# Attention unit in groups of three score steps and two split steps, and a second SBUF region moved to the first one's remainder by 512 bytes

## The chip, the cores and the metric

The kernel runs on one core of one Trainium2 chip. TensorE (PE in the profile) multiplies matrices, ScalarE (ACT) evaluates functions such as exp, VectorE (DVE) works elementwise, GpSimd (POOL) helps out, SyncE (SP) issues DMAs. The metric is the device time of one execution in microseconds. A kernel and its change are compared by the median of several executions.

## What is computed

One transformer block on `x` of 2 x 2048 tokens with 576 channels, conditioned by a vector per batch item. Cut to what matters here:

```python
h = modulate(rmsnorm(x, g1, D), scale_msa, shift_msa)
qkv = (h @ qkv_w.T + qkv_b).reshape(B, N, 3, 16, 36).transpose(2, 0, 3, 1, 4)
q, k, v = rmsnorm(qkv[0]) * 36 ** -0.5, rmsnorm(qkv[1]), qkv[2]
attn = softmax(einsum('bhqd,bhkd->bhqk', q, k))
o = einsum('bhqk,bhkd->bhqd', attn, v)
x = x + tanh(gate_msa) * (o @ proj_w.T + proj_b)
h2 = modulate(rmsnorm(x, g2, D), scale_mlp, shift_mlp)
x = x + tanh(gate_mlp) * (gelu(h2 @ fc1_w.T + fc1_b) @ fc2_w.T + fc2_b)
```

## The kernel before, in words

Everything is float32. A product that TensorE takes in its fast float32 form (fp32r) is made of two or three passes over a high and a low part of each operand, so most matmuls come as `hi` and `lo`.

There are three stages. The first makes q, k and v and stores them. The second, attention, ends at about 1882 us together with the first two output projections. The third, the feed-forward, runs over `NB` = 8 blocks of 512 tokens, and in each over 18 steps of a `fc1` and a `fc2`.

**A unit of attention** is one pair of heads against 512 queries; there are `NU` = 64, written out one after the other. It has 16 key steps `kt` of 128 keys.

- `score(u, kt)`, L1633: two matmuls (one for each head), weights from `kT`, moving operand `qT`, into one of `RING` = 3 slots of two PSUM banks. Before its first weight load it waits in `ring_free` until the exp of three entries earlier is done, since that exp reads the slot which the score overwrites.
- `exps(u, kt)`, L1248, on ScalarE, in the order of `kt`: one exp of 128 x 1024 out of the slot, into `p_r` for the eight split steps (`kt` 0 to 3 and 12 to 15) and into `prob` for the eight whole steps (4 to 11). Before the exp of step 6 ScalarE also copies out one half of the last unit's output (`take_ob`).
- `high_p`, `low_p`, L1446 and L1453, on VectorE: make `p_hi` and `p_lo` of a split step.
- `split_value(u, j)`, L1659: four matmuls of fp32r, weights `vx`, moving `p_hi` and `p_lo`; it waits for `low_p`, and the one with `j` = 0 also for the copies of the last unit's output (`take_oa`, `take_ob`), whose PSUM banks it restarts.
- `value(u, kt)`, L1649: two matmuls in full float32 for a whole step, all eight in a row at the unit's end.

The first four split steps of a unit (`j` 0 to 3) are multiplied in the unit itself, the last four in the next unit (`older(j)`). The order of all this on TensorE is the order of the calls in the loop `for u in range(NU)`; no scheduler moves anything. Semaphores alone tie the engines together. Around units 60 to 62 the projection of the first block (`proj(0, m)`) stands in between and takes a ring entry of its own.

**Memory.** `main_phase` lays its tensors in two regions of SBUF. The low one begins at `low_end` = 2816 bytes of each partition: `kT`, `vp`, `qT`, `prob`, and in the feed-forward `mh_hi`, `mh_lo`, `w1_hi`, `w1_lo`, `a_hi`, `a_lo`. The high one begins at `W2`, counted down from the top (`top` = 229312): the feed-forward weights `w2`, and in attention in the same place `p_hi`, `p_r`, `p_lo` and `vx`; below it, counted down from `W2`, the projection's weights `wp_hi`, `wp_lo` and inputs `o_hi`, `o_lo`. `low_end` leaves 256 when divided by 512, `W2` = 146368 leaves 448. The sizes of the tensors that the fp32r matmuls read, and the steps between their slices, are multiples of 512 bytes, so the whole high region reads at 448 and the low one at 256. In `fc2` (L1719) the weights lie in the high region and the moving operand in the low one.

Of the kernel before, what the change touches and what calls it, by code (L numbers as in the profile page):

```python
# [15 lines left out]
B, N, D = 2, 2048, 576  # L16
# [9 lines left out]
NT = N // P  # L26
FC = F // P
# [17 lines left out]
def wait(eng, sem, value):  # L45

    if isinstance(value, int) and value <= 0:
        return
    eng.wait_ge(sem, value)
# [33 lines left out]
def build(nc, xT, cT, ada, adan, adab, wqkv, qkvb, wp, pb, w1, f1b, w2, f2b, gains, outT):  # L83
# [7 lines left out]
    with ExitStack() as ctx:  # L91
        ps = ctx.enter_context(nc.psum_tensor("ps", [P, 8, 512], F32))

        def sb(stack, name, shape, dt=F32):
            return stack.enter_context(nc.sbuf_tensor(name, shape, dt, align_bytes=64 if np.prod(shape[1:]) >= P else 32))

        ident = sb(ctx, "ident", [P, P])
        ones = sb(ctx, "ones", [P, P], F32R)
        mod = sb(ctx, "mod", [P, 6, KC, B])
        gate_b = sb(ctx, "gate_b", [P, 2, KC, B])  # L100
        gain = sb(ctx, "gain", [P, 4])
        qscale = sb(ctx, "qscale", [P, 1])
        bound = sb(ctx, "bound", [P, 1])
        unbounded = sb(ctx, "unbounded", [P, 1], mybir.dt.int32)
        pb_t = sb(ctx, "pb_t", [P, KC])
        f2b_t = sb(ctx, "f2b_t", [P, KC])
        f1b_t = sb(ctx, "f1b_t", [P, FC])

        first = FirstUnit(nc, ctx, qk_hi, qk_lo, v_s, m_s)
        parts = qkv_phase(nc, ctx, sb, ps, first, xT, cT, ada, adan, adab, wqkv, qkvb, pb, f1b, f2b, gains, qk_hi, qk_lo, v_s, m_s,  # L110
                  ident, ones, mod, gate_b, gain, qscale, bound, unbounded, pb_t, f2b_t, f1b_t)
        main_phase(nc, ctx, ps, first, parts, qk_hi, qk_lo, v_s, m_s, l_s, oh_s, ol_s, xT, w2, wp, w1, outT, ident, ones, unbounded, bound, mod, gate_b,
                   gain, f1b_t)
# [720 lines left out]
def place(u):  # L834

    return u // C // B, u // C % B, u % C


def ring_of_step(n):

    return n + sum(n >= b for b in PROJ_BEFORE)
# [15 lines left out]
def main_phase(nc, ctx, ps, first_unit, parts, qk_hi, qk_lo, v_s, m_s, l_s, oh_s, ol_s, xT, w2, wp, w1, outT, ident, ones, unbounded, bound, mod, gate_b,  # L857
# [4 lines left out]

    top = nc.sbuf_top // 64 * 64
    low_end = first_unit.base
    W2 = top - 8 * FC * D
    WP = W2 - 4 * 2 * KC * DP
    OB = WP - 4 * (KC + KF) * BLK
    here = [low_end]

    def at(name, shape, dt, offset):  # L870
        return nc.alloc_sbuf_tensor_at(name, shape, dt, offset=offset)
# [5 lines left out]

    w2c = at("w2", [P, FC, 2 * D], F32R, W2)
    w2_raw = at("w2_raw", [P, FC, 2 * D], F32, W2)
    wp_hi = at("wp_hi", [P, KC, DP], F32R, WP)  # L880
# [4 lines left out]

    p_hi = at("p_hi", [P, HIGHS, 2 * BLK], F32R, W2)
    p_r = at("p_r", [P, NS, 2 * BLK], F32, W2 + 8 * HIGHS * BLK)
    p_lo = at("p_lo", [P, NS, 2 * BLK], F32R, W2 + 8 * HIGHS * BLK)
    VX = W2 + 8 * (HIGHS + NS) * BLK
# [170 lines left out]
    with nc.Block() as block:  # L1060
# [560 lines left out]
        def _(pe):  # L1621
            parts[4](pe)

            def ring_free(entry):

                before = entry - RING
                for m in range(KC):
                    if before == ring_of_proj(m):
                        pe.wait_ge(pgate_done, m + 1)
                        return  # L1630
                wait(pe, exp_done, before + 1 - sum(before > ring_of_proj(m) for m in range(KC)))

            def score(u, kt):  # L1633

                it, r, c = place(u)
                entry = ring_of_step(NT * u + kt)
                if kt == 0:
                    pe.wait_ge(q_ld[u % 2], QDMA * (u // 2 + 1))
                if u == 0 and kt == 2:
                    pe.wait_ge(first_unit.tqlo_done, B * NT)  # L1640
                if c == 0 and kt % TPB == 0:
                    pe.wait_ge(k_ld[r][kt // TPB], KDMA * (it + 1))
                ring_free(entry)
                for h in range(2):
                    mm = pe.matmul(ps[:, 2 * (entry % RING) + h, :], kT[r][:, h, kt * P:(kt + 1) * P], qT[:, u % 2, h],  # L1645
                                   start=True, stop=True)
                mm.then_inc(s_mm, 1)

            def value(u, kt):  # L1649

                it, r, c = place(u)
                j = kt - EARLY
                if c == 0 and j == 0:
                    pe.wait_ge(v_ld[r], 16 * (it + 1))
                pe.wait_ge(exp_done, NT * u + kt + 1)
                pe.matmul(OA[0:64], vp[r][:, kt, 0:64], prob[:, j, 0:BLK], start=False, stop=False)  # L1656
                pe.matmul(OBK[64:VW], vp[r][:, kt, 64:VW], prob[:, j, BLK:2 * BLK], start=False, stop=False).then_inc(fv_mm, 1)  # L1657

            def split_value(u, j):  # L1659

                r, q = u // C % B, NS * u + j
                if u % C == 0 and j == 0:
                    pe.wait_ge(v_split, 4 * (u // C + 1))
                if j == 0:
                    wait(pe, oa_evac, u)
                    wait(pe, ob_evac, u)
                pe.wait_ge(plo_done, q + 1)
                for h, out in enumerate((OA, OBK)):
                    for n, part in enumerate((p_hi[:, q % HIGHS], p_lo[:, j])):
                        mm = pe.matmul(out, vx[r][:, j, h], part[:, h * BLK:(h + 1) * BLK],  # L1670
                                       start=j == 0 and n == 0, stop=j == NS - 1 and n == 1)
                mm.then_inc(rv_mm, 1)

            def proj(i, m):

                if m == 0:
                    pe.wait_ge(o_ld, ODMA * (i + 1))
                if i == 0:
                    ring_free(ring_of_proj(m))
                elif i == 1 and m < 2:  # L1680
                    pe.wait_ge(exp_done, NT * NU)
                elif m == 0 and i > 1:
                    pe.wait_ge(nrm_done, i)
                elif m > 0:
                    pe.wait_ge(pgate_done, KC * i + m - (1 if i == 1 else 0))
                for k in range(KC):
                    parts = passes(k, wp_hi, wp_lo, o_hi, o_lo)
                    if m == KF:
                        parts = ((wp_hi, o_hi), (wp_hi, o_lo)) if k < KF else ((wp_hi, o_hi),)
                    for n, (w, a) in enumerate(parts):  # L1690
                        mm = pe.matmul(proj_bank(i, m), w[:, k, m * P:(m + 1) * P], a[:, k],  # L1691
                                       start=k == 0 and n == 0, stop=k == KF and n == len(parts) - 1)
                mm.then_inc(proj_mm, 1)
# [47 lines left out]
            for u in range(NU):  # L1741
                def older(j):

                    if u > 0:
                        split_value(u - 1, EARLY + j)

                score(u, 0)
                score(u, 1)
                older(0)
                score(u, 2)  # L1750
                older(1)
                score(u, 3)
                score(u, 4)
                older(2)
                score(u, 5)
                older(3)
                if u in (LAST + 1, LAST + 2):
                    proj(0, 2 * (u - LAST) - 1)
                for kt in range(6, 9):
                    score(u, kt)  # L1760
                split_value(u, 0)
                score(u, 9)
                split_value(u, 1)
                score(u, 10)
                score(u, 11)
                split_value(u, 2)
                if LAST <= u < LAST + 3:
                    if u == LAST:
                        pe.wait_ge(wplo_done, 2 * KC)
                    proj(0, 2 * (u - LAST))  # L1770
                score(u, 12)
                score(u, 13)
                split_value(u, 3)
                score(u, 14)
                score(u, 15)
                for kt in WHOLE:
                    value(u, kt)
            sum_rows(0)
# [76 lines left out]
```

## Time and profile before

| | |
|---|---|
| median of 3 executions | 2906.13 us (2906.03 to 2906.17) |
| the profiled execution | 2906.52 us |
| its span, first to last instruction | 2904.7 us |
| PE busy | 2880.2 us, 99% |
| DVE busy | 1968.6 us, 68% |
| ACT busy | 1578.1 us, 54% |
| granted TensorE clock, mean | 0.997 |

The profile's page has six parts: busy time of each engine, the span in 40 slices, DMA queues, the chain of work that ended last, the costliest groups of instructions, and DMA issues. The trace behind it answers in more detail; the view used most below is the timeline, where a row gives the start in us, the time from the first start to the last end, the engine, the line, the operation, the operands and how many instructions were merged. Matmuls overlap in it: the row's time holds all starts but one and the whole length of the last matmul, so the distance from the start of one row to the start of the next is what the matmuls took up of TensorE.

### The profile page before, as it was taken

The page shows a single profiled execution, that of the slowest core. Times are in us where ns is not written, and L with a number is a line of the kernel's source. Part 1 is how long each engine was busy: PE and PEld are TensorE (multiplying, and loading weights), DVE is VectorE, ACT ScalarE, POOL GpSimd, SP SyncE. Part 2 cuts the span into 40 slices and gives each one's busy share as a digit, 9 for nine tenths or more (in the row PEclk, how much of TensorE's full clock was granted, in tenths as well). Part 3 has the DMA queues.
Part 4 walks back from the last instruction along what each step waited for, and adds up shares of the span by engine and source line. Part 5 has one row for each costly group of instructions (what it writes and reads, how often), then busy time and mean ns, then how long its engine had stood idle before and what let it go on. Part 6 is the DMA issues. An engine that isn't in the chain of part 4 may idle for free.

```text
span 2904.7 us, 35301 instructions
## 1 busy us (share of the span) xinstructions
PE 2880.2 (99%) x12990; PEld 2175.9 (75%) x12990; DVE 1968.6 (68%) x2727; ACT 1578.1 (54%) x1924; POOL 213.3 (7%) x161
## 2 busy tenths in 40 slices
PE   8999999999999999999999999999999999999999
PEld 7999986666666666666666666788888888888887
DVE  7777778899888888888888887844344243424342
ACT  4334336776776677677677666634344343434342
POOL 1323310101000000000000000090000000000000
PEclk9999999999999999999999999999999999999999
DMA  6555554221322322222222223432222222322121
GB/s 229 164 190 171 176 172 131 87 77 59 88 74 77 85 76 63 81 80 78 76 80 68 74 84 92 137 122 86 74 86 74 82 78 87 98 90 87 41 69 50
DMA packets 238454, 282.67 MB, mean 97 GB/s; under 512 B 34960, under 2 KB 144016, under 8 KB 237392
## 3 DMA queue, kind: packets, MB, share of 16 engines
q1 hardware_dynamic: 233408, 270.80, 30.4%
q10 hardware_dynamic: 4880, 9.70, 1.0%
q8 instruction: 99, 1.62, 0.2%
q14 instruction: 67, 0.55, 0.1%
HBM read 195.50 MB, written 84.67 MB: 96 GB/s over the span
## 4 chain that ended last, share of the span: by engine, by line
PE 94%; DVE 3%; ACT 1%; DMA 1%; issue 0%; SPq 0%; POOL 0%; POOLq 0%; DVEq 0%; ACTq 0%
PE ps L1645 16%; PE ps L1670 16%; PE ps L1733 15%; PE ps L1715 15%; PE ps L1657 13%; PE ps L794 12%; PE ps L1691 4%; PE ps L1656 2%; PE ps L749 1%; ACT gated L1314 1%; DMA gain<-kg 0%; DVE p_lo L1457 0%; DVE x L1517 0%; PE ps L741 0%; DVE w_lo L1510 0%
## 5 line engine op out<-in xcount | busy, mean ns | idle before, releaser
L1258 ACT ACTIVATE p_r<-ps 128x1024 f32<-128x1024 f32 x512 | 491.8, 1025 | 406.4 <-PE ps L1645 406.4
L1457 DVE TENSOR_TENSOR p_lo<-p_r,p_hi 128x1024 fp32r<-128x1024 f32 x512 | 613.7, 1220 | 0.0
L1645 PE MATMUL ps<-qT,kT 110*128 110x512 f32 x2048 | 574.7, 398 | 2.8 <-DMA kT<-qk_hi_scratch 1.7
L1645 PEld LDWEIGHTS ps<-qT,kT 110*128 110x128 f32 x2048 | 382.8, 190 | 137.7 <-issue 51.4
L1258 ACT ACTIVATE prob<-ps 128x1024 f32<-128x1024 f32 x512 | 483.5, 1031 | 3.1 <-PE ps L1645 2.8
L1656 PE MATMUL ps<-prob,vp 128*64 128x512 f32 x1024 | 453.1, 595 | 0.0
L1657 PE MATMUL ps<-prob,vp 128*37 128x512 f32 x1024 | 451.7, 594 | 0.0
L1587 DVE TENSOR_TENSOR a_lo<-act,a_hi 128x512 fp32r<-128x512 f32 x144 | 101.6, 706 | 508.2 <-ACT a_hi L1301 508.2
L1451 DVE CAST p_hi<-p_r 128x1024 fp32r<-128x1024 f32 x512 | 350.5, 695 | 135.7 <-ACT p_r L1258 134.2
L1733 PE MATMUL ps<-a_hi,w 128*128 128x512 f32 x1296 | 415.4, 393 | 0.0
L1670 PE MATMUL ps<-p_hi,vx 128*128 128x512 f32 x1024 | 404.3, 395 | 0.1
L1670 PE MATMUL ps<-p_lo,vx 128*128 128x512 f32 x1024 | 403.2, 394 | 0.0
L1299 ACT ACTIVATE act<-ps,f1b_t 128x512 f32<-128x512 f32 x144 | 99.2, 689 | 505.0 <-PE ps L1715 503.5
L1657 PEld LDWEIGHTS ps<-prob,vp 128*37 128x37 f32 x1024 | 111.5, 114 | 247.7 <-issue 247.7
L1715 PE MATMUL ps<-mh_hi,w_hi 128*128 128x512 f32 x720 | 282.4, 392 | 2.0 <-DVE w_lo L1510 2.0
L1733 PEld LDWEIGHTS ps<-a_hi,w 128*128 128x128 f32 x1296 | 243.4, 188 | 52.6
L1733 PE MATMUL ps<-a_lo,w 128*128 128x512 f32 x720 | 280.6, 390 | 0.0
L1715 PE MATMUL ps<-mh_hi,w_lo 128*128 128x512 f32 x720 | 280.0, 389 | 0.0
L1670 PEld LDWEIGHTS ps<-p_hi,vx 128*128 128x128 f32 x1024 | 192.7, 188 | 46.1 <-issue 1.7
L1670 PEld LDWEIGHTS ps<-p_lo,vx 128*128 128x128 f32 x1024 | 193.7, 189 | 43.1
L1715 PE MATMUL ps<-mh_lo,w_hi 128*128 128x512 f32 x576 | 224.8, 390 | 0.0
L794 PE MATMUL ps<-w_hi,h_hi 128*128 128x432 f32 x640 | 181.9, 365 | 3.5 <-DVE h_lo L526 3.5
(194 smaller groups left out, 3556.0 us busy)
## 6 DMA issues: line engine op xcount, KB each, us to landing
w_raw<-w SPq DMA_DIRECT2D x144, 320.0 KB, 2.9
qk_hi_scratch<-aw SPq DMA_DIRECT2D x32, 576.0 KB, 3.2
qk_lo_scratch<-aw SPq DMA_DIRECT2D x32, 576.0 KB, 4.4
kT<-qk_hi_scratch SPq DMA_DIRECT2D x128, 144.0 KB
qT<-qk_hi_scratch SPq DMA_DIRECT2D x128, 144.0 KB
v_scratch<-stv SPq DMA_DIRECT2D x32, 512.0 KB, 2.7
vp<-v_scratch SPq DMA_DIRECT2D x16, 1024.0 KB, 9.2
xb<-xT SPq DMA_DIRECT2D x8, 1280.0 KB, 10.9
```

Source lines behind the costliest of these rows:

```text
L794: mm = pe.matmul(ps[:, q, 0:PIECE], a[:, r, k, cols], w[:, k, q * PIECE:(q + 1) * PIECE], start=k == 0 and n == 0, stop=k == KF and n == 1)
L1258: act.activation(out, ps[:, 2 * slot:2 * slot + 2, :].rearrange("p a b -> p (a b)"), ACT.Exp).then_inc(exp_done, 1)
L1451: dve.tensor_copy(p_hi[:, q % HIGHS], p_r[:, j]).then_inc(phi_done, 1)
L1457: dve.tensor_tensor(p_lo[:, j], p_r[:, j], f32(p_hi[:, q % HIGHS]), ALU.subtract).then_inc(plo_done, 1)
L1587: dve.tensor_tensor(a_lo[:, slot], act32[:, slot], f32(a_hi[:, slot]), ALU.subtract).then_inc(alo_done, 1)
L1645: mm = pe.matmul(ps[:, 2 * (entry % RING) + h, :], kT[r][:, h, kt * P:(kt + 1) * P], qT[:, u % 2, h], start=True, stop=True)
L1656: pe.matmul(OA[0:64], vp[r][:, kt, 0:64], prob[:, j, 0:BLK], start=False, stop=False)
L1657: pe.matmul(OBK[64:VW], vp[r][:, kt, 64:VW], prob[:, j, BLK:2 * BLK], start=False, stop=False).then_inc(fv_mm, 1)
L1670: mm = pe.matmul(out, vx[r][:, j, h], part[:, h * BLK:(h + 1) * BLK], start=j == 0 and n == 0, stop=j == NS - 1 and n == 1)
L1691: mm = pe.matmul(proj_bank(i, m), w[:, k, m * P:(m + 1) * P], a[:, k], start=k == 0 and n == 0, stop=k == KF and n == len(parts) - 1)
L1715: mm = pe.matmul(ps[:, 5 + slot, :], w[:, slot, c], a[:, i % 2, c], start=c == 0 and n == 0, stop=c == KF and n == 1)
L1733: mm = pe.matmul(ps[:, m, :], w, a[:, slot], start=k == 0 and n == 0, stop=k == FC - 1 and n == len(parts) - 1)
```

## The change

In the unit, the calls stand in another order, the same number of them. In memory, `W2` goes down from 146368 to 146176, so that it leaves 256 by 512 like `low_end`; everything that is counted from `W2` goes down by the same 192 bytes.

```diff
-    W2 = top - 8 * FC * D
+    W2 = low_end + (top - 8 * FC * D - low_end) // 512 * 512
@@ the unit, in the loop over u @@
-                score(u, 0)
-                score(u, 1)
+                for kt in range(3):
+                    score(u, kt)
                 older(0)
-                score(u, 2)
                 older(1)
-                score(u, 3)
-                score(u, 4)
+                for kt in range(3, 6):
+                    score(u, kt)
                 older(2)
-                score(u, 5)
                 older(3)
...
                 for kt in range(6, 9):
                     score(u, kt)
                 split_value(u, 0)
-                score(u, 9)
                 split_value(u, 1)
-                score(u, 10)
-                score(u, 11)
-                split_value(u, 2)
+                for kt in range(9, 12):
+                    score(u, kt)
                 if LAST <= u < LAST + 3:
...
                     proj(0, 2 * (u - LAST))
                 score(u, 12)
-                score(u, 13)
+                split_value(u, 2)
                 split_value(u, 3)
-                score(u, 14)
-                score(u, 15)
+                for kt in range(13, NT):
+                    score(u, kt)
                 for kt in WHOLE:
                     value(u, kt)
```

Only TensorE's order changes; VectorE, ScalarE, GpSimd and the DMA queue keep theirs. In the rows below `L1645` is a matmul of a score and `L1670` one of a split step. First the start of the second unit, before and then after: two scores and one split step, against three scores and the first of two split steps.

```order
L1645 MATMUL ps<-qT,kT_49 128x512 [waits m_exp_done,m_q_ld1]
L1645 MATMUL ps<-qT,kT_49 128x512
L1645 MATMUL ps<-qT,kT_49 128x512 [waits m_exp_done]
L1645 MATMUL ps<-qT,kT_49 128x512
L1670 MATMUL ps<-p_hi,vx_62 128x512 [waits m_plo_done]
L1670 MATMUL ps<-p_lo,vx_62 128x512
L1670 MATMUL ps<-p_hi,vx_62 128x512
L1670 MATMUL ps<-p_lo,vx_62 128x512
L1645 MATMUL ps<-qT,kT_49 128x512 [waits m_exp_done]
L1645 MATMUL ps<-qT,kT_49 128x512
```

```order
L1645 MATMUL ps<-qT,kT_49 128x512 [waits m_exp_done,m_q_ld1]
L1645 MATMUL ps<-qT,kT_49 128x512
L1645 MATMUL ps<-qT,kT_49 128x512 [waits m_exp_done]
L1645 MATMUL ps<-qT,kT_49 128x512
L1645 MATMUL ps<-qT,kT_49 128x512 [waits m_exp_done]
L1645 MATMUL ps<-qT,kT_49 128x512
L1670 MATMUL ps<-p_hi,vx_62 128x512 [waits m_plo_done]
L1670 MATMUL ps<-p_lo,vx_62 128x512
L1670 MATMUL ps<-p_hi,vx_62 128x512
L1670 MATMUL ps<-p_lo,vx_62 128x512
L1670 MATMUL ps<-p_hi,vx_62 128x512 [waits m_plo_done]
```

Score 2 moved ahead of the first split step. The second place is around score 12, on TensorE in the same unit. Before, scores 10 and 11 stand here, then split step 2, then scores 12 and 13:

```order
L1645 MATMUL ps<-qT,kT_49 128x512 [waits m_exp_done]
L1645 MATMUL ps<-qT,kT_49 128x512
L1645 MATMUL ps<-qT,kT_49 128x512 [waits m_exp_done]
L1645 MATMUL ps<-qT,kT_49 128x512
L1670 MATMUL ps<-p_hi,vx_62 128x512 [waits m_plo_done]
L1670 MATMUL ps<-p_lo,vx_62 128x512
L1670 MATMUL ps<-p_hi,vx_62 128x512
L1670 MATMUL ps<-p_lo,vx_62 128x512
L1645 MATMUL ps<-qT,kT_49 128x512 [waits m_exp_done]
L1645 MATMUL ps<-qT,kT_49 128x512
L1645 MATMUL ps<-qT,kT_49 128x512 [waits m_exp_done]
L1645 MATMUL ps<-qT,kT_49 128x512
```

After, the end of split step 1, then scores 9, 10, 11 and 12, then split step 2:

```order
L1670 MATMUL ps<-p_hi,vx_62 128x512
L1670 MATMUL ps<-p_lo,vx_62 128x512
L1645 MATMUL ps<-qT,kT_49 128x512 [waits m_exp_done]
L1645 MATMUL ps<-qT,kT_49 128x512
L1645 MATMUL ps<-qT,kT_49 128x512 [waits m_exp_done]
L1645 MATMUL ps<-qT,kT_49 128x512
L1645 MATMUL ps<-qT,kT_49 128x512 [waits m_exp_done]
L1645 MATMUL ps<-qT,kT_49 128x512
L1645 MATMUL ps<-qT,kT_49 128x512 [waits m_exp_done]
L1645 MATMUL ps<-qT,kT_49 128x512
L1670 MATMUL ps<-p_hi,vx_62 128x512 [waits m_plo_done]
L1670 MATMUL ps<-p_lo,vx_62 128x512
```

So one group has four scores in a row, the others three. By `ring_free`, score 12 waits for the exp of step 9, which is the first score of its own group.

## Rows read from the trace of the kernel before

**Rows 1.** The page: busy times, granted clock by slice, chain by engine.
```profile
PE 2880.2 (99%) x12990; PEld 2175.9 (75%) x12990; DVE 1968.6 (68%) x2727; ACT 1578.1 (54%) x1924; POOL 213.3 (7%) x161
...
PEclk9999999999999999999999999999999999999999
...
PE 94%; DVE 3%; ACT 1%; DMA 1%; issue 0%; SPq 0%; POOL 0%; POOLq 0%; DVEq 0%; ACTq 0%
```
**Rows 2.** Windows, units 1 to 59: us, busy and instructions by engine, clock.
```profile
461.70:1759.20 1297.50, 1297.36 (x5667) 844.49 (x5665) 1146.19 (x1532) 910.56 (x1003) 21.95 (x15) 1.00 0.27 78
```
**Rows 3.** Timeline of PE, one unit: start, us, line, operands, number of matmuls.
```profile
1407.72 1.20 PE L1645 MATMUL ps<-qT,kT 110*128 110x512 f32 x4
1408.76 0.40 PE L1670 MATMUL ps<-p_hi,vx 128*128 128x512 f32 x1
...
1411.09 1.07 PE L1645 MATMUL ps<-qT,kT 110*128 110x512 f32 x4
1411.99 0.39 PE L1670 MATMUL ps<-p_hi,vx 128*128 128x512 f32 x1
...
1414.31 1.52 PE L1645 MATMUL ps<-qT,kT 110*128 110x512 f32 x6
1415.67 0.39 PE L1670 MATMUL ps<-p_hi,vx 128*128 128x512 f32 x1
...
1417.99 1.07 PE L1645 MATMUL ps<-qT,kT 110*128 110x512 f32 x4
...
1421.68 1.07 PE L1645 MATMUL ps<-qT,kT 110*128 110x512 f32 x4
1422.68 0.64 PE L1656 MATMUL ps<-prob,vp 128*64 128x512 f32 x1
```
**Rows 4.** Timeline of PE, split steps and projection; 58 matmuls stand between.
```profile
1868.47 0.39 PE L1670 MATMUL ps<-p_lo,vx 128*128 128x512 f32 x1
...
1881.85 0.39 PE L1691 MATMUL ps<-o_hi,wp_hi 128*128 128x512 f32 x1
```
**Rows 5.** Timeline of PE, one step of the feed-forward: fc1 (L1715), fc2 (L1733).
```profile
2152.59 0.40 PE L1715 MATMUL ps<-mh_hi,w_hi 128*128 128x512 f32 x1
...
2155.78 0.62 PE L1733 MATMUL ps<-a_hi,w 128*128 128x512 f32 x2
...
2158.99 0.40 PE L1715 MATMUL ps<-mh_hi,w_hi 128*128 128x512 f32 x1
```
**Rows 6.** Timeline of ACT in the unit of rows 3.
```profile
1411.74 1.02 ACT L1258 ACTIVATE p_r<-ps 128x1024 f32<-128x1024 f32 x1 [0.35 <-PE ps L1645]
...
1415.00 5.59 ACT L1258 ACTIVATE prob<-ps 128x1024 f32<-128x1024 f32 x6
1420.50 3.77 ACT L1258 ACTIVATE p_r<-ps 128x1024 f32<-128x1024 f32 x4
```
**Rows 7.** Timeline of DVE in the unit of rows 3.
```profile
1412.81 1.22 DVE L1457 TENSOR_TENSOR p_lo<-p_r,p_hi 128x1024 fp32r<-128x1024 f32 x1
1414.51 0.69 DVE L1404 COPY oa<-ps 101x512 f32<-101x512 f32 x1 [0.48 <-PE ps L1670]
...
1415.72 2.35 DVE L1457 TENSOR_TENSOR p_lo<-p_r,p_hi 128x1024 fp32r<-128x1024 f32 x2
```
**Rows 8.** Timeline in unit 63, where scores wait for an exp.
```profile
1842.81 3.75 ACT L1258 ACTIVATE p_r<-ps 128x1024 f32<-128x1024 f32 x4
...
1844.78 0.73 PE L1645 MATMUL ps<-qT,kT 110*128 110x512 f32 x2 [0.19 <-ACT p_r L1258]
...
1845.35 0.40 PE L1670 MATMUL ps<-p_hi,vx 128*128 128x512 f32 x1
```

## The prediction

> **What bounds the kernel now.** I read the page first: PE is busy 99% of the span, the chain of what ended last is 94% PE, and the granted clock is at its upper level, 2.4 GHz, in practically all of it [rows 1]. In units 1 to 59 PE has no gap at all (1297.36 of 1297.50 us), while DVE and ACT have slack [rows 2]. So TensorE's queue is the time, and the change, which reorders that queue and moves what it reads, can act in two ways only: through the distance between two matmuls, and through a wait that opens a gap. The view for both is the timeline.
>
> The distance is not the same everywhere. The least is 0.2267 us: the 59 distances from 1868.47 to 1881.85 take 13.38 us [rows 4]. Those matmuls, split steps and projection mixed, all read the high region, weights and moving operand alike. The six score matmuls from 1414.31 to 1415.67, which all read the low region, take 1.36 us, the same 0.2267 [rows 3]. But where the two alternate it is more. From 1411.99 to 1414.31 stand ten matmuls (split step, score, split step) in 2.32 us, where ten at 0.2267 are 2.27; from 1415.67 to 1417.99 it is the same again [rows 3]. Over the unit: from 1407.72 to 1422.68 are 14.96 us for 64 matmuls [rows 3]. The first costs 0.34 (four in 1.04 us, of which I take about 0.02 as an after-effect), the last 0.32 (1421.68 plus three at 0.2267 is 1422.36, and the next starts at 1422.68), and 62 at 0.2267 are 14.06, in all 14.72. **So 0.24 us of a unit of some 22 us are excess**, and they go with the change of region.
>
> The feed-forward shows it as well: one step, 14 matmuls of fc1 and 14 of fc2, takes 6.40 us from 2152.59 to 2158.99, where 28 at 0.2267 are 6.35 [rows 5]. The excess is 0.05 us. There fc2 mixes a weight of the high region with a moving operand of the low one.
>
> **The move in memory.** It adds no instruction. The regions differ in where they lie and in their remainder by 512 (256 and 448). The rows can't separate the two. For the remainder speaks the size: the excess of ten matmuls across two round trips of regions is 0.05 us, and 512 bytes are 128 elements, which at 2.4 GHz are 0.053 us, as if reads had to come round to a place in a 512-byte line. With equal remainders I take the excess to be gone, except after a restart (after the value steps, 0.02 us in each unit).
> - Attention: (0.24 - 0.02) x 64 = 14.1 us less; the new wait below makes one more restart in each unit, 0.02 x 64 = 1.3 us, so 12.8 us less.
> - Feed-forward: 0.053 x 144 steps = 7.6 us less [rows 5]; the steps near block ends, with projections between, I count the same.
> - Bounds: nothing at all if it is the place and not the remainder; 0.24 x 64 + 7.6 = 23.0 us if all goes. A loss I exclude, since streams with equal remainders on both operands run at the least distance in both regions [rows 3, 4].
>
> Against this stands the Trainium skill, "TensorE: Matmul & The Clock Gate", Part 1 (the section on 56 ns against 53.3): back-to-back matmuls at the upper clock are a fixed N / 2.4 GHz + 2.5 ns apart, whatever they read, 0.216 us for 512 columns. The trace has 0.227 and more, so the figure does not hold for these operands. By the rule the move in memory would be worth nothing, and the time would be that of the second case below, which is priced from rows.
>
> **The order: what moves at no cost.** Grouping halves the changes of region from 16 to 8 in a unit. If the move in memory already takes the excess away, this is worth nothing more; if not, half of 0.21, about 0.10 us a unit, 6.7 us in all. What each moved call waits for:
> - The older split steps 0 to 3 were ready units ago on DVE. Split step 1 now starts about 8.7 us into the unit (0.34 + 37 x 0.2267) instead of 9.4; its `p_lo` is done at 1414.03, 6.3 us in [rows 7]. Split step 2 starts later than before and its `p_lo` is done by 1418.07 [rows 7].
> - Split step 0 waits for the copy of the last unit's output, done at 1415.20 [rows 7], against a start at 1415.67 [rows 3]. Twelve matmuls of scores and sixteen of split steps precede the copy in both orders, and six of scores follow, so the margin stays.
> - Each score waits for the exp of three steps before. An exp starts 0.42 us after the second matmul of its score (1411.32 to 1411.74) and lasts 1.02 [rows 3, 6]; exps in a run start every 0.914 us (5.59 less 1.02, over five) [rows 6]. The tightest places in the new order, in us from the unit's start: score 5 asks at about 3.9 for the exp of step 2, over at about 3.6 (the first starts at 0.77, two more follow); score 8 asks at 7.1 for that of step 5, which ends at 6.8 (step 3's second matmul is the sixteenth, at 3.5, plus 0.42, two more starts and 1.02). Both hold.
>
> **The order: what costs.** Score 12 now follows scores 9, 10 and 11 directly, and its ring slot is the one that the exp of step 9 reads. Before, split steps 1 and 2, eight matmuls or 1.8 us, stood between 9 and 12. Count from *a*, the start of score 9's second matmul, unhindered: score 12 would start five matmuls later, at a + 1.13. The exp of step 9 starts at a + 0.42, if ACT is free. It is: the run of exps 6 to 11 would have its fourth at 1415.00 + 3 x 0.914 = 1417.74 [rows 6], while score 9 now comes after two split steps, its second matmul at 1415.67 + 9 x 0.2267 = 1417.71, plus 0.42 is 1418.13. So the exp ends at a + 1.44. In unit 63 the same wait is to be seen: the second of four exps ends at 1842.81 + 0.91 + 1.02 = 1844.74, and the waiting score starts at 1844.78 [rows 8]. So score 12 starts at a + 1.44 + 0.05 = a + 1.49, 0.36 late. Its weights could not be loaded ahead either: in unit 63 the two matmuls of the released score take 1845.35 - 1844.78 = 0.57 us instead of 0.45 [rows 8], 0.12 more. **The wait costs 0.48 us in each unit.** Nothing covers it: behind the waiting load, PE's queue holds score 12 and the split steps 2 and 3, whose operands are ready but stand behind it.
>
> Does it come back later? Score 15 waits for the exp of step 12. Without the stop at 12 that exp would come late: a + 0.42 + 3 x 0.914 + 1.02 + 0.05 = a + 4.23, and the weight load wants to start 18 matmuls after a, at a + 4.08. With the stop everything on PE is 0.48 later while exp 12 moves by less, and the margin is there. So the stop swallows that one, and nothing else is late. In units 60 to 62 a projection stands between 11 and 12; its ring entry waits for the same exp, so the price is the same there. 64 x 0.48 = **30.7 us more**. Bounds: 0.36 us (no loss in the reload, 23.0 us in all) and 0.57 (0.09 more, the time by which such an exp in rows 8 could end later than I read it, 36.5 us).
>
> **The sum.** Against the profiled execution, 2906.5 us: + 30.7 - 12.8 - 7.6 = + 10.3. The median of the runs lies 0.4 lower: 2906.1 + 10.3 = 2916.4 us, 0.35% slower.
>
> **The cases.**
> 1. The above: 2916.4, with the terms' spread 2909 to 2921. Chance 0.58.
> 2. The excess belongs to the place, not to the remainder; then the order's wait stays and only the fewer changes of region help: 2906.1 + 30.7 - 6.7 = 2930.1. For it: no row has two remainders inside one region. Against it: the size of the step. Chance 0.24. Between the two lies a part of the effect (for instance in attention alone), 2917 to 2925, chance 0.06.
> 3. Faster. The mechanism is that the exp of step 9 is not the last thing that score 12 waits for in effect: the place is score 12's weight load, and it decides when the exp is over before a + 0.91, when that load would start. Then 30.7 us fall away, what is left is the late load of score 15 (0.15 us late; a load may slip a little before it shows, so at most 0.1 x 64 = 6 us), and the time is 2906.1 - 20.4 + up to 6, 2886 to 2892. Against it: exp and release add up to 1.49 us, and rows 8 show the wait in the same form. Chance 0.06.
> 4. A second wait that I don't see, for example the copy before split step 0 slipping past its margin, 0.1 us a unit on top of case 1 or 2: 2923 to 2937, chance 0.06.
>
> **How the numbers follow.** Likeliest is case 1: 2916.4. The range takes case 1 and 2: 2909 to 2932, about 0.85 of the chance by the cases. A measurement of this kernel can tell about 0.2% (5.8 us) from no change: that is 2900.3 to 2911.9. Faster 0.06, same 0.07 (the low end of case 1), slower 0.87.
>
> **What would show it.** In the waits view PE's L1645 should wait for ACT's exp into `prob` some 60 times at about 0.2 us each (0.36 late, less the tail of the matmul before), 12 to 13 us in sum, where there was nothing. In the timeline of a unit two scores' worth of matmuls after score 9 a released pair should take 0.57 us. If the remainder is the cause, ten matmuls across regions take 2.27 us, not 2.32, and a feed-forward step 6.35, not 6.40; if it is the place, both stay. A unit should take 21.97 + 0.48 - 0.20, about 22.25 us, in case 1 and 22.35 in case 2. I am wrong if PE shows no gap in the units: then case 3.

## The result, and the profile after

The changed kernel takes **2931.19 us** (median of four runs, 2930.62 to 2931.87). The kernel before, run beside it, takes 2906.15 us. The ratio is 1.0085, with a 95% interval of 1.0072 to 1.0097. So it is slower by 25.0 us, where 10.3 were forecast. The time lies inside the range, and 1.1 us from the number of the second case. The experiments show that this second case is nevertheless not the cause. So it is luck that the range holds it.

The page of the changed kernel answers [rows 1]. First the busy times by engine, then the shares of the chain, then the group of the score matmuls, whose last column is the idle time ahead of them and what ended most of it:

```profile
PE 2887.6 (99%) x12990; PEld 2167.1 (74%) x12990; DVE 1975.3 (67%) x2727; ACT 1588.3 (54%) x1924; POOL 213.5 (7%) x161
...
PE 93%; ACT 3%; DVE 2%; DMA 1%; issue 1%; SPq 0%; POOL 0%; POOLq 0%; ACTq 0%; DVEq 0%
...
L1645 PE MATMUL ps<-qT,kT 110*128 110x512 f32 x2048 | 553.1, 402 | 17.2 <-ACT prob L1258 13.6
```

ACT has entered the chain with 3%, because scores now wait for an exp. The waits of PE (total us, times, longest) name it:

```profile
PE ps L1645 <- ACT prob L1258: 13.6, 61, 0.3
PE ps L1691 <- ACT prob L1258: 0.7, 3, 0.3
```

Those are one wait in each of the 64 units; in units 60 to 62 the projection stands in the waiting place (L1691). Over units 1 to 59, which answer to [rows 2], the window reads (us, then busy us and instructions of PE, PEld, DVE, ACT and POOL, granted clock, DMA share, GB/s):

```profile
463.20:1788.89 1325.69, 1312.40 (x5666) 838.03 (x5664) 1151.70 (x1532) 919.91 (x1003) 21.94 (x15) 1.00 0.26 77
```

These 59 units take 28.2 us more than before. PE's idle time in them went from 0.14 to 13.29 us. The other 15.0 us are busy time for the same matmuls, 0.25 us a unit, so half of the loss is not seen as a gap at all: what follows shows 0.12 of it in the pair behind the wait, and the rest is the end of the matmul ahead of the gap, under which 0.36 us of lateness become 0.22 of idle time. The clock is at its upper level throughout, as before.

The timeline of PE in one unit of the changed kernel (start, us, line, operands, number of matmuls) shows where this lies:

```profile
1117.04 0.40 PE L1670 MATMUL ps<-p_hi,vx 128*128 128x512 f32 x1
...
1118.88 1.55 PE L1645 MATMUL ps<-qT,kT 110*128 110x512 f32 x6
1120.27 0.40 PE L1670 MATMUL ps<-p_hi,vx 128*128 128x512 f32 x1
...
1125.34 1.55 PE L1645 MATMUL ps<-qT,kT 110*128 110x512 f32 x6
1127.09 0.73 PE L1645 MATMUL ps<-qT,kT 110*128 110x512 f32 x2 [0.20 <-ACT prob L1258]
1127.66 0.39 PE L1670 MATMUL ps<-p_hi,vx 128*128 128x512 f32 x1
```

**The wait.** Scores 9 to 11 start at 1125.34. The second matmul of score 9 comes 0.23 us later, at 1125.57. Plus 0.42 that makes 1125.99 for the exp, and the timeline of ACT has it at 1126.00:

```profile
1126.00 2.86 ACT L1258 ACTIVATE prob<-ps 128x1024 f32<-128x1024 f32 x3 [0.35 <-PE ps L1645]
```

It ends some 1.02 later, at 1127.02, and score 12 starts at 1127.09. The released pair takes 1127.66 - 1127.09 = 0.57 us.

**The distances.** Eight matmuls of split steps and six of scores, from 1117.04 to 1120.27, take 3.23 us, where fourteen at 0.2267 are 3.17. Six scores from 1118.88 take 1.39 us instead of 1.36. The remainders by 512 are now equal, and the excess is still there. The feed-forward, on the other hand, has lost its excess: the step that answers to [rows 5] takes 2189.42 - 2183.08 = 6.34 us, where it took 6.40.

```profile
2183.08 0.39 PE L1715 MATMUL ps<-mh_hi,w_hi 128*128 128x512 f32 x1
...
2186.25 0.62 PE L1733 MATMUL ps<-a_hi,w 128*128 128x512 f32 x2
...
2189.42 0.39 PE L1715 MATMUL ps<-mh_hi,w_hi 128*128 128x512 f32 x1
```

By the starts of the matmuls, attention (from the start of the first unit to 0.52 us behind the start of the last value matmul) went from 1426.7 to 1458.7 us. The rest after it, up to the start of the last matmul, went from 1036.5 to 1029.6, which is 7.0 us back before rounding.

### The profile page after: what moved, and what is told of

It is laid out like the page before. It is cut to its first block, busy times and chain, and to the rows that moved or that the text cites. A ratio compares the mean times of both kernels' runs of the same rounds, so it can differ in the third digit from the quotient of the medians.

```text
span 2930.1 us, 35301 instructions
## 1 busy us (share of the span) xinstructions
PE 2887.6 (99%) x12990; PEld 2167.1 (74%) x12990; DVE 1975.3 (67%) x2727; ACT 1588.3 (54%) x1924; POOL 213.5 (7%) x161
## 4 chain that ended last, share of the span: by engine, by line
PE 93%; ACT 3%; DVE 2%; DMA 1%; issue 1%; SPq 0%; POOL 0%; POOLq 0%; ACTq 0%; DVEq 0%
PE ps L1670 16%; PE ps L1645 15%; PE ps L1715 15%; PE ps L1733 15%; PE ps L1657 13%; PE ps L794 12%; PE ps L1691 4%; ACT prob L1258 2%; PE ps L1656 2%; PE ps L749 1%; ACT gated L1314 1%; DMA gain<-kg 0%; DVE x L1517 0%; PE ps L741 0%; DVE w_lo L1510 0%
## 5 line engine op out<-in xcount | busy, mean ns | idle before, releaser
L1258 ACT ACTIVATE p_r<-ps 128x1024 f32<-128x1024 f32 x512 | 498.3, 1029 | 406.9 <-PE ps L1645 406.9
L1645 PE MATMUL ps<-qT,kT 110*128 110x512 f32 x2048 | 553.1, 402 | 17.2 <-ACT prob L1258 13.6
L1645 PEld LDWEIGHTS ps<-qT,kT 110*128 110x128 f32 x2048 | 377.1, 189 | 174.0 <-issue 61.7
L1733 PE MATMUL ps<-a_hi,w 128*128 128x512 f32 x1296 | 410.8, 389 | 0.0
L1670 PE MATMUL ps<-p_lo,vx 128*128 128x512 f32 x1024 | 402.2, 393 | 0.0
L1670 PE MATMUL ps<-p_hi,vx 128*128 128x512 f32 x1024 | 402.0, 393 | 0.2
L1715 PE MATMUL ps<-mh_hi,w_hi 128*128 128x512 f32 x720 | 281.1, 390 | 2.4 <-DVE w_lo L1510 2.4
L1733 PEld LDWEIGHTS ps<-a_hi,w 128*128 128x128 f32 x1296 | 243.2, 188 | 51.0
L1733 PE MATMUL ps<-a_lo,w 128*128 128x512 f32 x720 | 280.2, 389 | 0.0
L1715 PE MATMUL ps<-mh_hi,w_lo 128*128 128x512 f32 x720 | 280.2, 389 | 0.0
L1670 PEld LDWEIGHTS ps<-p_hi,vx 128*128 128x128 f32 x1024 | 192.5, 188 | 46.0 <-issue 1.8
L1670 PEld LDWEIGHTS ps<-p_lo,vx 128*128 128x128 f32 x1024 | 193.0, 188 | 43.7
L1715 PE MATMUL ps<-mh_lo,w_hi 128*128 128x512 f32 x576 | 224.1, 389 | 0.0
```

Of the source, the lines that this page charges most:

```text
L1258: act.activation(out, ps[:, 2 * slot:2 * slot + 2, :].rearrange("p a b -> p (a b)"), ACT.Exp).then_inc(exp_done, 1)
L1715: mm = pe.matmul(ps[:, 5 + slot, :], w[:, slot, c], a[:, i % 2, c], start=c == 0 and n == 0, stop=c == KF and n == 1)
L1733: mm = pe.matmul(ps[:, m, :], w, a[:, slot], start=k == 0 and n == 0, stop=k == FC - 1 and n == len(parts) - 1)
```

## The experiments

Beside the time of each kernel, the table has two numbers from its trace: the median unit (start of one unit's first score to that of the next) and the rest behind attention. The kernel before was run again beside each group of experiments; its median was 2906.15, 2906.67, 2906.41 and 2906.53 us, and each ratio is against the one beside it.

| kernel | median us | against before (95%) | unit, us | rest, us |
|---|---|---|---|---|
| before | 2906.15 | | 21.97 | 1036.5 |
| after | 2931.19 | 1.0085 (1.0072 to 1.0097) | 22.44 | 1029.6 |
| move_only | 2904.89 | 0.9993 (0.9984 to 1.0003) | 22.05 | 1029.6 |
| order_only | 2938.08 | 1.0108 (1.0091 to 1.0124) | 22.43 | 1036.5 |
| split2_first | 2902.25 | 0.9984 (0.9975 to 0.9994) | 22.01 | 1029.6 |
| rows128_after | 2920.61 | 1.0047 (1.0031 to 1.0064) | 22.27 | 1029.6 |
| rows128_move | 2886.00 | 0.9927 (0.9910 to 0.9943) | 21.74 | 1029.7 |
| rows128_before | 2905.78 | 0.9995 (0.9986 to 1.0005) | 21.95 | 1036.5 |
| rows128_split2 | 2890.94 | 0.9943 (0.9927 to 0.9960) | 21.81 | 1029.6 |
| rows128_rem384 | 2909.44 | 1.0010 (1.0000 to 1.0019) | 21.92 | 1042.1 |
| five_in_a_row | 2956.24 | 1.0169 (1.0140 to 1.0199) | 22.89 | 1029.6 |
| split110_after | 2921.56 | 1.0052 (1.0029 to 1.0075) | 22.27 | 1029.7 |

The theory formed from the two traces, A in what was expected, is this. The wait before score 12 costs about 0.5 us in each unit. Equal remainders do take the feed-forward's excess away. In attention the excess stays, because scores read 110 rows and split steps 128, and a change of the number of rows disturbs the stream by itself. In the kernel before, each change of region between scores and split steps is also a change of the number of rows, so its rows could not tell the two apart.

### The move alone

The order of the kernel before, with only this line:

```diff
-    W2 = top - 8 * FC * D
+    W2 = low_end + (top - 8 * FC * D - low_end) // 512 * 512
```

> Only the high region moved to the remainder 256, the order of before. Theory A (what the trace after suggests): the move frees the feed-forward alone, 7.0 us, and attention keeps its excess at every change between scores and split steps, whose cause is something else: 2899 us, at most 2905 if the 16 short groups cost more than before. Rival B (the move also frees attention in this order, and it was the new order that brought the excess back): 7.0 + 12.8 less, 2886 us. Rival C (the move is worth nothing in either): 2906.

Measured: 2904.89 us, 1.8 us less than the 2906.67 of the kernel before beside it. The feed-forward gives its 7.0 us back. The unit goes from 21.97 to 22.05, up by 0.09, and 64 of those take 5.5 back. So the move, thought to be good for 20 us, is worth nothing that can be told from no change. In attention, equal remainders alone make it slightly worse.

### The order alone

The order of the changed kernel, `W2 = top - 8 * FC * D` as before.

> Only the order changed, the high region at 448 as before. Theory A: the wait before score 12 costs 0.48 x 64 = 30.7 us, the fewer changes of group give little back, and the feed-forward is as before: 2931.2 + 7.0 = 2938 us, 0.24 us of excess a unit as before. Rival (fewer changes of region are worth 0.10 us a unit): 2930 to 2932 us.

Measured: 2938.08 us, against the 2938 that A gives. The unit is 22.43 us, and 22.44 with the move, so in the new order too the move takes nothing out of attention. The wait is the same too:

```profile
PE ps L1645 <- ACT prob L1258: 14.0, 61, 0.3
```

The two parts add up: + 31.4 for the order and - 1.8 for the move make + 29.6, where both together gave + 25.0. The rest of 4.6 us is about the 0.09 us a unit (5.5 us) that the move costs in the old order and not in the new.

### The changed kernel without its wait

Split step 2 goes back between scores 9 to 11 and score 12. Everything else, the coarser groups included, is as in the changed kernel:

```diff
                 for kt in range(9, 12):
                     score(u, kt)
+                split_value(u, 2)
 ...
                 score(u, 12)
-                split_value(u, 2)
                 split_value(u, 3)
```

> The changed kernel with split step 2 put back ahead of score 12, so that no group has four scores. If the ring wait at score 12 is what costs: 30 us less, plus up to 6 us for the late weight load of score 15, 2901 to 2907 us, and the gap before score 12 is gone from the waits view. Rival (the coarser groups cost by themselves, for instance by holding up VectorE or ScalarE): above 2920 us.

Measured: 2902.25 us, 28.9 less than the changed kernel, and just below the kernel before. PE has no wait for an exp into `prob` any more. In its timeline the six matmuls of scores 9 to 11 take 1.39 us (1419.26 up to split step 2 at 1420.65). Then comes split step 2, and score 12 follows without a stop:

```profile
1419.26 1.55 PE L1645 MATMUL ps<-qT,kT 110*128 110x512 f32 x6
1420.65 0.40 PE L1670 MATMUL ps<-p_hi,vx 128*128 128x512 f32 x1
...
1421.58 0.63 PE L1645 MATMUL ps<-qT,kT 110*128 110x512 f32 x2
...
1422.97 1.56 PE L1645 MATMUL ps<-qT,kT 110*128 110x512 f32 x6
```

One step in another place is the whole difference between slower by 25 us and not slower. Against move_only, which has the old order in the same memory, split2_first is 2.6 us less (unit 22.01 against 22.05). The intervals of the two overlap, so the coarser groups alone gain little, if anything.

### The wait twice

Score 13 follows 12 directly, so scores 9 to 13 stand in a row:

```diff
                 score(u, 12)
+                score(u, 13)
                 split_value(u, 2)
                 split_value(u, 3)
-                for kt in range(13, NT):
+                for kt in range(14, NT):
```

> The changed kernel with score 13 moved up as well, so that scores 9 to 13 stand in a row. If the price is the ring wait, a second one of the same kind follows: score 13 waits for the exp of step 10, ready at a + 0.42 + 0.91 + 1.02 + 0.05 = a + 2.40, where it would start at 2.06 after the first stop, plus 0.12 for the reload: 0.46 us more in each unit, 2960 us, with twice as many waits of PE for the exp into prob, some 120. Rival (one stop lets ScalarE catch up, so the second costs little): 2931 to 2940 us.

Measured: 2956.24 us, 25 us above the changed kernel; 2960 was expected. The median unit is 0.45 us longer, with two stops:

```profile
PE ps L1645 <- ACT prob L1258: 21.7, 107, 0.3
...
1413.74 0.73 PE L1645 MATMUL ps<-qT,kT 110*128 110x512 f32 x2 [0.20 <-ACT prob L1258]
1414.65 0.74 PE L1645 MATMUL ps<-qT,kT 110*128 110x512 f32 x2 [0.18 <-ACT prob L1258]
```

The view lists 107 of these waits, where some 120 were expected: 15 second gaps are shorter (about 0.12 us) and not listed, and units 60 to 62, where a projection stands between scores 11 and 12, have no second gap. They last 25.71, 29.03 and 27.95 us, no longer than in the changed kernel (25.72, 29.09 and 27.93). In the other units up to 59 the second stop costs about as much as the first. From one released score to the next are 0.91 us, the distance of exps in a run [rows 6], where two matmuls at 0.2267 would be 0.45: once the scores catch up with the exps they go at ACT's pace.

### Scores that read 128 rows, in the changed kernel

The tiles `kT` and `qT` get 128 partitions instead of 110. The added rows hold ones in `kT` and zeros in `qT`, so that they add nothing to a score. GpSimd writes them before attention; the second `kT` tensor and the ones of the first are changed in the same way:

```diff
-        self.kT = nc.alloc_sbuf_tensor_at("kT0", [PKW, 2, N], F32R, offset=base)
+        self.kT = nc.alloc_sbuf_tensor_at("kT0", [P, 2, N], F32R, offset=base)
-        self.qT = nc.alloc_sbuf_tensor_at("qT", [PKW, 2, 2, BLK], F32R, offset=base + 8 * N + 4 * NT * VP)
+        self.qT = nc.alloc_sbuf_tensor_at("qT", [P, 2, 2, BLK], F32R, offset=base + 8 * N + 4 * NT * VP)
 ...
+        pool.memset(f32(first_unit.qT[96:P]), 0.0).then_inc(q_zero, 1)
 ...
-            pool.memset(f32(kT[1][96:PKW]), 1.0).then_inc(kones, 1)
+            pool.memset(f32(kT[1][96:P]), 1.0).then_inc(kones, 1)
```

> The changed kernel, but the score matmuls read 128 partitions of kT and qT instead of 110 (the 18 added rows are ones against zeros, so the scores are the same). Theory A: the excess at each change between scores and split steps comes from the change of the number of rows, 110 against 128, since split steps and projection, both of 128 rows, change without any. Then 8 changes x 0.026 us x 64 units = 13.3 us less, 2918 us, and score and split distances are 0.2267 us throughout. Rival (it comes from other tensors, banks or accumulation flags of the two kinds): 2931 us, same distances. Rival 2 (more rows take longer to read): above 2931 us.

Measured: 2920.61 us, 10.6 less than the changed kernel; 2918 was expected. The matmuls read more and take less time. In the timeline six scores start at 1119.93 and take 1.52 us to the end of the last, where they took 1.55. Ahead of the stop, all distances from scores to split steps and back are 0.2267:

```profile
1119.93 1.52 PE L1649 MATMUL ps<-qT,kT 128*128 128x512 f32 x6
1121.66 0.73 PE L1649 MATMUL ps<-qT,kT 128*128 128x512 f32 x2 [0.21 <-ACT prob L1262]
```

Here the wait can be read in a clean stream: score 12 would start at 1119.93 + 6 x 0.2267 = 1121.29 and starts at 1121.66, 0.37 late.

### The same number of rows, but 110

In the changed kernel the split steps read 110 rows as well. This leaves the last 18 keys of each split step out of the sum, so part of the computation is missing:

```diff
-                        mm = pe.matmul(out, vx[r][:, j, h], part[:, h * BLK:(h + 1) * BLK],
+                        mm = pe.matmul(out, vx[r][0:PKW, j, h], part[0:PKW, h * BLK:(h + 1) * BLK],
```

> The changed kernel, but the matmuls of the split steps read 110 partitions instead of 128, like the scores; it leaves out the share of the last 18 keys of each split step. If it is the change of the number of rows that disturbs, and not 110 as such: scores and split steps change without excess, 0.21 us less in each unit, 2918 us, as with 128 rows on both. If 110 rows by themselves are slower, or the kinds of matmul differ in some other way: 2931 us or more.

Measured: 2921.56 us, the unit 22.27 us as with 128 everywhere. The scores that took 1.39 us up to the next split step take 1.36 again:

```profile
1117.86 1.52 PE L1645 MATMUL ps<-qT,kT 110*128 110x512 f32 x6
1119.22 0.39 PE L1670 MATMUL ps<-p_hi,vx 110*128 110x512 f32 x1
```

So it isn't that 110 rows are slow, or that fewer are faster. What costs is the change from one number to the other. In these kernels the weights and the moving operand of a matmul always change together, so which of the two matters isn't shown.

### The move and 128 rows, in the order of before

> The order of before, the region moved to remainder 256, and scores of 128 rows. Theory A (a change of row count and a change of remainder both disturb the distances; with neither, none is left): a unit of 21.97 less all its excess of 0.23 us, 21.73 us, so 2904.9 (move alone) less 0.32 x 64 = 20.4: 2884.5 us. Rival (the short groups cost by themselves): 2895 us or more.

Measured: **2886.00 us**, ratio 0.9927 (0.9910 to 0.9943). This is the fastest kernel of the study, 20.4 us below the kernel before beside it and 45 below the changed one. A stretch of the densest alternation, sixteen matmuls of scores and split steps from 1405.14 to 1408.76, takes 3.62 us, 0.2263 each:

```profile
1405.14 1.52 PE L1649 MATMUL ps<-qT,kT 128*128 128x512 f32 x6
1406.50 0.39 PE L1674 MATMUL ps<-p_hi,vx 128*128 128x512 f32 x1
...
1407.40 0.62 PE L1649 MATMUL ps<-qT,kT 128*128 128x512 f32 x2
...
1408.76 1.07 PE L1649 MATMUL ps<-qT,kT 128*128 128x512 f32 x4
```

The unit is 21.74 us, 0.23 less than before. That is the excess of 0.24 that the prediction had read from [rows 3].

### 128 rows without the move

The same, with `W2 = top - 8 * FC * D` as before.

> The order of before, the region at 448 as before, only the scores read 128 rows. Theory A: the rows are alike now but the remainders are not, so the 16 changes of region in a unit still disturb, about as in before (0.23 us a unit), and the feed-forward keeps its 7 us: 2906 us, between 2898 and 2908. Rival (in attention only the row count mattered, and the remainder matters in the feed-forward alone): 14.7 us less than before, 2892 us.

Measured: 2905.78 us, ratio 0.9995 (0.9986 to 1.0005), no change. With the three others in the order of before this makes a square (unit, us):

| | 110 and 128 rows | 128 rows everywhere |
|---|---|---|
| remainders 256 and 448 | 21.97 | 21.95 |
| remainders both 256 | 22.05 | 21.74 |

Neither condition alone is worth anything in attention. Both together are worth 0.23 us a unit. The remainder is worth 0.21 us a unit (13 us in all) where the rows agree, and less than nothing where they don't.

### 128 rows, the new groups, no wait

The edit of split2_first on top of rows128_after.

> The changed kernel with split step 2 ahead of score 12 and scores of 128 rows: groups of three, but the last two shorter. With no excess left, units run faster than ScalarE's chain allows at score 15, whose weight load comes 0.15 to 0.18 us late: 21.73 + 0 to 0.1 us a unit, 2884 to 2891 us, at or above the order of before under the same conditions. Rival (coarser groups gain something of their own): below 2884 us.

Measured: 2890.94 us, 4.9 above rows128_move, unit 21.81 against 21.74. Once the stream is clean the coarser groups bring nothing and cost a little. The row that shows it is a weight load, score 15's, that comes late for the exp of step 12, as the prediction had reckoned for a kernel without the stop:

```profile
1416.27 0.30 PEld L1649 LDWEIGHTS ps<-qT,kT 128*128 128x128 f32 x2 [0.21 <-ACT p_r L1262]
```

It costs 0.07 us a unit; the prediction had at most 0.1.

### Another difference of remainders

rows128_move, with the high region at remainder 384 instead of 256, so that the difference is 128 bytes instead of none:

```diff
+    W2 = low_end + (top - 8 * FC * D - low_end) // 512 * 512 + 128
```

> As rows128_move, but the high region leaves 384 by 512 against 256 of the low one, a difference of 128 bytes, and it lies only 128 bytes from where it stood there. If what counts is the remainder by 512: excess comes back in both stages, feed-forward 3 to 8 us and attention up to 15 us, 2890 to 2906 us. If a difference of 128 is as good as none (the remainder by 128 counts): 2884.5 us, as rows128_move.

Measured: 2909.44 us, 23.4 above rows128_move: by the two traces 10.0 in attention (unit 21.92) and 12.4 in the rest. The fourteen fc2 matmuls of a step take 3.25 us (2157.76 - 2154.51), where 14 x 0.2267 are 3.17:

```profile
2154.51 0.64 PE L1737 MATMUL ps<-a_hi,w 128*128 128x512 f32 x2
...
2157.76 0.39 PE L1719 MATMUL ps<-mh_hi,w_hi 128*128 128x512 f32 x1
```

So it is the remainder and not the place: the region moved by 128 bytes. Whether it is the remainder by 512 or by 256 isn't shown, since no run has a difference of 256. A longer period is unlikely: the weights of successive scores lie 512 bytes apart, and in rows128_move all of them run at the least distance. A difference of 128 costs the feed-forward more than one of 192 did (12.4 us against 7.0), so the price doesn't grow with the difference.

## Why the prediction was right or wrong

**What bounds the kernel: right.** TensorE's queue is the time, and the change acted through the two ways named, distances and a gap.

**The wait: right.** 0.36 us late and 0.12 in the released pair were forecast, 0.48 us a unit. The lateness is 0.37 us in the clean stream of rows128_after, and the pair takes 0.57 us as [rows 8] had it. In whole units the changed order costs 22.27 - 21.74 = 0.53 us between the two kernels of 128 rows. It contains the longer distances behind the restart, for which the prediction counted 0.02 apart. Between the changed kernel and split2_first it is 22.44 - 22.01 = 0.43. Both lie within 0.05 of 0.48. The 12 to 13 us in about 60 waits were 13.6 in 61. The third case, that score 12 wouldn't wait in effect, falls: taking away what makes it wait gave 28.9 us.

**Feed-forward: right.** 7.6 us were forecast and 7.0 measured, in each kernel that has the move. The step went from 6.40 to 6.34, forecast 6.35.

**Attention, the excess: wrong, and this is the step that failed.** "With equal remainders I take the excess to be gone" gave - 12.8 us; nothing came back. The cleanest evidence is the pair order_only and after, which differ in the move alone: 22.43 and 22.44 us a unit. Attention grew by 32.0 us, where + 30.7 - 12.8 = + 17.9 was forecast. Of the 14.1 us between, 12.8 are this term. The other 1.3 are units 0 and 63, which grew by 1.1 us each instead of 0.48; what in them cost more wasn't followed. Unit 0 lasts between 24.7 and 25.9 us in the five kernels with the old order, so its part may be chance. The size of the excess was right (0.24 forecast to be there, 0.23 gone in rows128_move), and so was its link to the remainder. What was missing is a second condition, the number of rows. It stands in the very rows that the argument used: "110*128 110x512" and "128*128 128x512" in [rows 3]. The prediction took from them only which region was read. [rows 4], the stream at the least distance across different operands, has 128 rows in every matmul, so it was no evidence for a stream that alternates between 110 and 128.

**"A loss I exclude": wrong as well.** For the move alone, each unit became 0.09 us longer.

**The second case: right number, wrong reason.** It had the excess belong to the place, with no gain in the feed-forward and 6.7 us from fewer changes of region. Instead the feed-forward gave 7.0. The order alone cost 22.43 - 21.97 = 0.46 us a unit. Set against the forecast 0.48 for the wait, the fewer changes gave 0.02 back instead of 0.10; set against the 0.53 of the kernels of 128 rows, 0.07. The runs don't divide this any further. One reason for a small gain is in the raw starts: there are half as many changes, but the longer distances last longer behind each. In order_only eight split-step matmuls in a row take 0.045 us more than at 0.2267, where four in a row take 0.02 more in the kernel before. The prediction set two rows as a test. The feed-forward step of 6.34 is what case 1 said; the unit of 22.44 is neither the forecast 22.25 nor 22.35. So case 1 held in the feed-forward, and neither case held in attention.

The Trainium skill was weighed in the prediction: "TensorE: Matmul & The Clock Gate", Part 1, has a fixed cost per matmul on top of N / 2.4 GHz, with no term for what is read. In the runs the least distance stayed 0.226 to 0.227 us and not 0.216, and the distance wasn't fixed: a region moved by 128 bytes added 23.4 us. The same page, Part 2, step 1, says that the row count doesn't matter for loading weights and that a load doesn't take read bandwidth from the running matmul. The first agrees with the traces: a score's weight load lasts 0.190 us on average with 110 rows (before) and 0.189 with 128 (rows128_move). Beside the second stands fc2, whose weights and moving operand lie in different regions: the feed-forward step lost 0.06 us when only the two remainders became equal. Whether the load or the moving operand was held up there, no row tells.

## What to carry to other kernels

When a stream of matmuls is the bound, look at what is the same and what differs between neighbours in every respect that the rows show (address, rows, shape) before an excess is put down to one of them; here two had to agree, and in attention a test of one alone showed no gain. Padding an operand so that all matmuls read the same number of rows can be free and gain time, although more is read. When steps are grouped, compare the length of each group with the ring of buffers that feeds it: three scores in a row fit this ring, and the fourth cost 0.43 to 0.53 us each time.

## What the runs showed of the hardware

- **Changing the number of rows.** After a change between 110 and 128 rows five distances are longer, 0.232, 0.236, 0.228, 0.233 and 0.231 us by the raw starts in the changed kernel; some 0.026 us in all. Then it is 0.2267 again. Staying at either number costs nothing. In the changed kernel it comes to 0.17 us a unit (22.44 - 22.27), where there are eight such changes. Six stand ahead of the stop, 0.16 us; the other two come behind it, where the distances are longer with 128 rows everywhere as well. Nearly the same row of distances (0.236, 0.228, 0.232, 0.231) stands behind the first score matmul of a unit in rows128_after, where the rows don't change. Why is not shown, and other numbers than 110 and 128 weren't tried.
- **The remainder by 512 bytes.** In the feed-forward, whose matmuls all read 128 rows, a difference of 192 bytes costs 7.0 us and one of 128 bytes 12.4 us. With 128 rows everywhere, regions with remainders 256 and 448 cost 19.8 us in all (2905.78 - 2886.00), and a difference of 128 bytes cost 23.4 us. Three differences (0, 128, 192) are too few for a rule, and the prediction's picture of reads that come round to a place in a line of 512 bytes stays a guess.
- **Two disturbances don't add.** With the number of rows changing, equal remainders cost 0.09 us a unit in the order of before and nothing in the new one. Why one hides the other is open.
